# Group means of a four-layer image kernel: from a matmul with a matrix of means to block turns and sums on VectorE

## The reference

```python
xg = x.reshape(B, H, W, GROUPS, C // GROUPS)
mean = jnp.mean(xg, axis=(1, 2, 4), keepdims=True)
var = jnp.var(xg, axis=(1, 2, 4), keepdims=True)
xg = (xg - mean) * jax.lax.rsqrt(var + EPS)
```

## Time and profile before

| | us |
|---|---|
| median of 3 runs | 160.66 |
| lowest and highest | 159.46, 163.44 |
| the profiled execution, its own time | 159.53 |
| its span in the trace | 157.7 |
| PE busy | 149.7 (95%) |
| DVE busy | 104.8 (66%) |
| ACT busy | 108.7 (69%) |
| POOL busy | 50.1 (32%) |

### The profile page before, as it was taken

One profiled execution on the slowest core, in us unless ns is written; L12 is line 12 of the kernel. 1 busy time (PEld: TensorE's weight loads), 2 busy tenths in 40 slices (PEclk: granted clock), 3 DMA queues, 4 the chain that ended last, 5 costly groups with the idle time before them and its releaser, 6 DMA issues.

```text
span 157.7 us, 3715 instructions
## 1 busy us (share of the span) xinstructions
PE 149.7 (95%) x1405; PEld 114.7 (73%) x1405; DVE 104.8 (66%) x265; ACT 108.7 (69%) x261; POOL 50.1 (32%) x115
## 2 busy tenths in 40 slices
PE   7989999999999999999989997999989999999992
PEld 4569889887777678766667765766677756799992
DVE  0577899999996898568956377639975611235543
ACT  3567979973688458983778942697358879567970
POOL 6467657534517442214020038010200050026100
PEclk9999999999999999999999999999999999999999
DMA  5960000000000000000000000000000020000003
GB/s 147 321 267 0 0 8 0 2 4 0 2 2 4 0 0 4 4 0 4 4 2 6 4 0 0 8 0 4 2 2 8 0 75 0 0 4 33 0 33 133
DMA packets 2800, 4.30 MB, mean 27 GB/s; under 512 B 352, under 2 KB 2272, under 8 KB 2784
## 3 DMA queue, kind: packets, MB, share of 16 engines
q1 hardware_dynamic: 2496, 3.87, 7.2%
q10 hardware_dynamic: 288, 0.21, 0.4%
HBM read 2.90 MB, written 1.05 MB: 25 GB/s over the span
## 4 chain that ended last, share of the span: by engine, by line
PE 71%; DVE 16%; ACT 5%; POOL 4%; issue 2%; DVEq 0%; ACTq 0%
PE psum L658 9%; PE psum L647 8%; PE psum L626 7%; DVE nmax L1148 6%; PE psum L573 4%; PE psum L553 3%; PE psum L685 3%; PE psum L699 3%; ACT pT L907 3%; PE psum L728 3%; PE psum L669 2%; PE psum L721 2%; PE psum L720 2%; PE psum L518 2%; PE psum L737 2%
## 5 line engine op out<-in xcount | busy, mean ns | idle before, releaser
L1148 DVE TENSOR_REDUCE nmax<-psum 128x4 f32<-128x1024 f32 x32 | 38.3, 1217 | 6.7 <-PE psum L626 6.7
L907 ACT ACTIVATE pT<-psum 128x1024 f32<-128x1024 f32 x32 | 31.6, 1027 | 4.7 <-PE psum L647 4.4
L626 PE MATMUL psum<-qk 16*128 16x256 f32 (+1 forms) x256 | 18.1, 397 | 0.0
L647 PE MATMUL psum<-qk 32*128 32x256 f32 (+1 forms) x256 | 18.0, 398 | 0.1
L332 POOL COPY zE<-zE 128x17 f32<-128x17 f32 x8 | 1.6, 198 | 46.1 <-ACT zE L924 46.1
L658 PE MATMUL psum<-pT,vaug_all 128*32 128x256 f32 x256 | 16.0, 383 | 0.0
L626 PEld LDWEIGHTS psum<-qk 16*128 16x128 f32 (+1 forms) x256 | 11.7, 184 | 4.4 <-DVE nmax L1148 1.5
L647 PEld LDWEIGHTS psum<-qk 32*128 32x128 f32 (+1 forms) x256 | 11.6, 184 | 3.9 <-issue 1.6
L326 POOL TENSOR_TENSOR rstd<-vare,half 128x1 f32<-128x1 f32 x16 | 9.5, 591 | 14.7 <-DVE vare L1101 14.7
L382 POOL TENSOR_SCALAR mv<-mv 128x1 f32<-128x1 f32 x16 | 6.0, 375 | 24.7 <-DVE mv L1088 24.6
L658 PEld LDWEIGHTS psum<-pT,vaug_all 128*32 128x32 f32 x256 | 7.3, 109 | 6.4 <-issue 2.2
(11 more groups left out here) (160 smaller groups left out, 352.5 us busy)
## 6 DMA issues: line engine op xcount, KB each, us to landing
out<-x SPq DMA_DIRECT2D x8, 128.0 KB, 1.9
tab<-in_weights SPq DMA_DIRECT2D x1, 708.0 KB, 7.8
tab<-in_weights SPq DMA_DIRECT2D x1, 576.0 KB, 5.4
x0T<-in_xT SPq DMA_DIRECT2D x4, 128.0 KB, 3.1
x0T<-in_xT_rest SPq DMA_DIRECT2D x1, 512.0 KB, 6.2
tab<-in_weights SPq DMA_DIRECT2D x1, 320.0 KB, 6.6
qk<-stage_all SPq DMA_DIRECT2D x16, 8.0 KB
tab<-in_weights ACTq DMA_DIRECT2D x1, 128.0 KB, 2.9
```

The source lines that it names most:

```text
L626: last = mm(bank[(b0, b1)[j // 2] + j % 2][:, u * TOK:(u + 1) * TOK], at[:, u, 0, :], at[:, :, 1, :], start=True, stop=True)
L647: last = mm(bank[(b0, b1)[j // 2] + j % 2][:, m * TOK:(m + 1) * TOK], at[:, m, 1, :], at[:, :, 0, :], start=True, stop=True)
L907: go(pT[g](i)[:, 2 * k:2 * k + 2].rearrange("p j m t -> p j (m t)"), pair(home["st", g, i][k]), ACT.Exp).then_inc(s["exp" + "EO"[g]], 1)
L1148: v.tensor_reduce(nmax2(i)[:, g, 2 * k:2 * k + 2, :], pair(home["sm", g, i][k]).rearrange("p j (u m) -> p j u m", u=TILES), AX.X, ALU.max, ...
```

## The change

The matrices `mean1` and `mean2` leave the table (128 columns each of the third and fourth load), and with them `gm1` and `gm2` leave PE. In their place DVE gets four calls per norm. `turned` transposes the 32 x 32 blocks of a 128 x 32 tile, of which only the two columns of mean and mean of squares hold data: each block of 32 channels comes to lie along the free dimension. `group_sum` adds over groups of 4 or 8 channels there, `group_scaled` divides by the size of the group, and `turned_back` reads each result 4 or 8 times over and transposes the blocks back, so that every channel has its group's values in SBUF tile `gm`. `variance` and `normalised` read that tile and no PSUM. The tile `mv` becomes 32 columns wide and is filled with zeros once. The bias of L2 is added as a sum of two tiles, the second a column read 256 times over. All five sequences and the choice of banks are written anew.

```diff
-        mv = [ring(f"mv{k}", [P, 2]) for k in (1, 2)]
+        mv_all = [sb(f"mv{k}", [P, SLOTS, 32]) for k in (1, 2)]
+        mv = [lambda i, k=k: mv_all[k][:, i % SLOTS] for k in range(2)]
+        mvT, gm = ([ring(f"{n}{k}", [P, 32]) for k in (1, 2)] for n in ("mvT", "gm"))
+        sumT, gT = ([ring(f"{m}{k + 1}", [P, 32 // n]) for k, n in enumerate((GROUP1, GROUP2))] for m in ("sumT", "gT"))
...
+                for k in range(2):
+                    gp.memset(mv_all[k][:, :, :], 0.0)
...
-                gp.tensor_scalar(x2b(i), x0T(i), b_out2[:, :], None, ALU.add).then_inc(s["x2b"], 1)
+                gp.tensor_tensor(x2b(i), x0T(i), b_out2[:, :].to_broadcast((P, TOK)), ALU.add).then_inc(s["x2b"], 1)
...
-            def gm1(i, *marks):
-                freed(*marks)
-                pe.wait_ge(s["ms1"], i + 1)
-                mm(bank[home["o0", i]][:, TOK:TOK + 2], w("mean1"), mv[0](i), start=True, stop=True).then_inc(s["gm1"], 1)
...
-            def gm2(i, *marks):
...
-                mm(bank[home["o1", i]][:, TOK:TOK + 2], w("mean2"), mv[1](i), start=True, stop=True).then_inc(s["gm2"], 1)
...
-                v.bn_aggr(mv[layer - 1](i), bn[layer - 1](i)).then_inc(s[f"mv{layer}"], 1)
+                v.bn_aggr(mv[layer - 1](i)[:, 0:2], bn[layer - 1](i)).then_inc(s[f"mv{layer}"], 1)
+
+            def turned(i, layer, *marks):
+                after(marks)
+                dve.wait_ge(s[f"ms{layer}"], i + 1)
+                v.transpose(mvT[layer - 1](i), mv[layer - 1](i)).then_inc(s[f"mvT{layer}"], 1)
+
+            def group_sum(i, layer, *marks):
+                after(marks)
+                dve.wait_ge(s[f"mvT{layer}"], i + 1)
+                n = (GROUP1, GROUP2)[layer - 1]
+                v.tensor_reduce(sumT[layer - 1](i), mvT[layer - 1](i).rearrange("p (k n) -> p k n", n=n), AX.X, ALU.add).then_inc(s[f"sumT{layer}"], 1)
+
+            def group_scaled(i, layer, *marks):
+                after(marks)
+                dve.wait_ge(s[f"sumT{layer}"], i + 1)
+                n = (GROUP1, GROUP2)[layer - 1]
+                v.tensor_scalar(gT[layer - 1](i), sumT[layer - 1](i), 1.0 / n, None, ALU.mult).then_inc(s[f"gT{layer}"], 1)
+
+            def turned_back(i, layer, *marks):
+                after(marks)
+                dve.wait_ge(s[f"gT{layer}"], i + 1)
+                n = (GROUP1, GROUP2)[layer - 1]
+                v.transpose(gm[layer - 1](i), gT[layer - 1](i).unsqueeze(2).to_broadcast((P, 32 // n, n))).then_inc(s[f"gm{layer}"], 1)
...
-                g = bank[home[f"o{layer - 1}", i]][:, TOK:TOK + 2]
+                g = gm[layer - 1](i)
...
-                mean_of_group = bank[home[f"o{k}", i]][:, TOK:TOK + 1]
-                v.tensor_scalar(xn[k](i), x0T(i), mean_of_group, rstd[k](i), ALU.subtract, ALU.mult
+                v.tensor_scalar(xn[k](i), x0T(i), gm[k](i)[:, 0:1], rstd[k](i), ALU.subtract, ALU.mult
```

More of the change, by code:

```diff
@@ L412, in _ @@
+            z_difference(7, ("a", 6)); z_sum(7)
         @block.tensor
@@ L792, in _ @@
+            om(4, 4, ("xout", 4)); om(5, 1, ("s3", 7)); om(6, 0); om(7, 4, ("xout", 5))
         @block.scalar
@@ L980, in _ @@
+            s3_out(4); s3_out(5); s3_out(6); s3_out(7, ("out_ps", 5))
         @block.vector
@@ new lines, in _ @@
+            group_scaled(0, 1); turned_back(0, 1); variance(0, 1); variance_eps(0, 1); turned(1, 1); nmax0_out(4)
+            sum0_out(3); values_folded(); normalised(0, 1); group_sum(1, 1); group_scaled(1, 1); x1_out(2)
+            turned_back(1, 1); variance(1, 1); variance_eps(1, 1); moments(2, 1); inv0_out(3); mean(2, 1); sum0_out(4)
+            normalised(1, 1); p0_scaled(3); inv0_out(4); turned(2, 1); p0_scaled(4); nmax1_out(0); mlp_folded()
+            nmax1_out(1); inv1_out(0); group_sum(2, 1); p1_scaled(0); x1_out(3); group_scaled(2, 1); moments(3, 1)
@@ new lines, in _ @@
+            turned_back(2, 1); variance(2, 1); variance_eps(2, 1); nmax0_out(5); pool0(7); inv1_out(1); mean(3, 1)
+            normalised(2, 1); p1_scaled(1); x2_out(0); moments(0, 2); mean(0, 2); sum0_out(5); turned(3, 1)
+            group_sum(3, 1); inv0_out(5); group_scaled(3, 1); turned(0, 2); turned_back(3, 1); group_sum(0, 2)
+            group_scaled(0, 2); turned_back(0, 2); variance(0, 2); variance_eps(0, 2); nmax1_out(2); variance(3, 1)
+            normalised(0, 2); x2_out(1); x1_out(4); variance_eps(3, 1); moments(1, 2); moments(4, 1); mean(1, 2)
@@ new lines, in _ @@
+            nmax0_out(6); inv1_out(2); normalised(3, 1); turned(1, 2); p1_scaled(2); group_sum(1, 2); out2_folded()
+            group_scaled(1, 2); turned_back(1, 2); mean(4, 1); p0_scaled(5); nmax2_out(0, 0, 0); variance(1, 2)
+            nmax2_out(0, 0, 1); variance_eps(1, 2); nmax1_out(3); turned(4, 1); normalised(1, 2); nmax2_out(0, 1, 0)
+            group_sum(4, 1); group_scaled(4, 1); nmax2_out(0, 1, 1); turned_back(4, 1); inv1_out(3); variance(4, 1)
+            variance_eps(4, 1); x2_out(2); p1_scaled(3); normalised(4, 1); nmax2_out(1, 1, 0); x1_out(5); sum0_out(6)
@@ new lines, in _ @@
+            moments(2, 2); inv0_out(6); p0_scaled(6); nmax2_out(1, 1, 1); moments(5, 1); mean(5, 1); mean(2, 2)
+            nmax1_out(4); turned(5, 1); group_sum(5, 1); turned(2, 2); group_scaled(5, 1); group_sum(2, 2)
+            group_scaled(2, 2); turned_back(2, 2); variance(2, 2); variance_eps(2, 2); x1_out(6); moments(6, 1)
+            normalised(2, 2); turned_back(5, 1); variance(5, 1); x2_out(3); inv1_out(4); variance_eps(5, 1)
+            moments(3, 2); p1_scaled(4); normalised(5, 1); mean(3, 2); nmax2_out(1, 0, 0); nmax2_out(1, 0, 1)
@@ new lines, in _ @@
+            turned(3, 2); group_sum(3, 2); nmax1_out(5); nmax2_out(2, 1, 0); group_scaled(3, 2); turned_back(3, 2)
+            x2_out(4); nmax2_out(2, 1, 1); nmax0_out(7); mean(6, 1); variance(3, 2); moments(4, 2); variance_eps(3, 2)
+            sum0_out(7); turned(6, 1); group_sum(6, 1); group_scaled(6, 1); turned_back(6, 1); inv0_out(7)
+            normalised(3, 2); p0_scaled(7); mean(4, 2); nmax2_out(2, 0, 0); oinv_out(0); on_out(0); turned(4, 2)
+            inv1_out(5); variance(6, 1); variance_eps(6, 1); nmax2_out(2, 0, 1); normalised(6, 1); x1_out(7)
```

242 lines of the change are left out of this document (110 added, 132 removed).

## The result

| | before | changed |
|---|---|---|
| median us | 159.53 | 161.20 |
| lowest and highest | 159.16, 163.44 | 160.84, 163.80 |
| executions | 16 | 16 |
| profiled execution, its span | 159.53, 157.7 | 161.26, 159.4 |

The changed kernel takes 1.0097 times as long, 95% interval 1.0072 to 1.0121: slower by 1.0%. The forecast was 159.6, against the 160.66 shown, and a profiled execution 1.0 us quicker than before's; it became 1.7 us slower.

A forecast was written before the change was run, and what follows sets the result against it. PE, busy 95% of 157.7 us, was taken to set the length, with DVE also full from 20 to 46 us. Span 56.5 + 99.4 + 2.2 - 0.4 - 1.0 = 156.7 us, execution 158.5, predicted median 159.6, range 155.5 to 163.5.

The forecast's parts named there:

- the 4.5 us for the calls: DVE up to the maxima of image 1: nine norms at 0.5 us more each, 4.5 us more work.
- No wait for `z_sum(1)`, 1.0 us: POOL: `z_sum(1)` directly after the difference ends the wait of `am(1)`, 1.0 us gained.
- The last maxima of image 1: DVE ahead of `nt(1)`: 56.0 + 2.7 more work - 2.3 of waits gone, so done at 56.4 us.
- No wait of PE for a transfer behind `nt(1)`: Between `nt(1)` and `st(1, 1)`: about 2.5 us of PE work covers the transfer, priced at 0, up to 1.4 in the range.
- the credits ahead of `nt(1)`: DVE up to the maxima of image 1: 2.3 us of waits gone and 1.8 us less of other work.
- `nt(1)` right behind the maxima, 56.5: PE at image 1: `nt(1)` starts at 56.5 us instead of 58.3, directly after DVE's last maxima.
- The cover behind `nt(1)`: From `nt(1)` to the end: additional DVE work mostly covered, read from DVE busy 32.9 of 60 us between 80 and 140.
- PE's removed work behind `nt(1)` and the bank, put at 1.4 us: PE behind `nt(1)`: five group matmuls take 1.0 us away, a bank wait ahead of an `o1` 0.4.
- The price per norm: DVE: four calls of 0.69 us, less 0.08 overlap and 0.13 for `variance`, cost 0.5 us more; bounds 0.3 to 1.2.
- The banks' 3 us behind `nt(1)`: Rival, chance 0.37: banks freed earlier remove 3 us more of PE's waits behind `nt(1)`; median 156.6, 2.5% faster.
- DVE as the bound up to image 3: Rival, chance 0.15: norms cost DVE 1.0 us or more each, `nt(1)` starts at 61.0, median 164.1, 2.1% slower.
- 3.2 us of matmuls: PE: sixteen group matmul calls at 0.2 us each leave, 2.2 us ahead of `nt(1)` and 1.0 behind.

The follow-up runs named there:

- The kernel without calls: Changed kernel without the four DVE calls of each norm, group means left out, against the changed kernel: 156.80 us, 0.9809 of before, span 155.0.
- the kernel with all norms by turns and freed banks: Kernel before, old order: group matmuls replaced by the four DVE calls, six PE bank waits on x1 or x2: 165.84 us, 1.038 of before, span 164.0.
- the one without calls, to which 1.0 is added: Kernel before, old order, without group matmuls or DVE calls, banks freed, `z_sum(1)` earlier: 157.77 us, 0.9888 of before, span 155.4.
- The calls on spare tiles: Kernel before, group matmuls kept, plus four dependent DVE calls on unread tiles behind each `normalised`: 167.34 us, 1.0501 of before, span 165.5.
- the kernel with four late norms by turns: Kernel before with earlier `z_sum(1)`, second norms of images 4 to 7 by the four DVE calls, their banks freed: 159.16 us, 0.9974 of before.
- The kernel with the projections moved: Changed kernel with L0 projections of images 4 and 5 moved behind `p0t(0)` and `fold_biases2` on PE: 163.91 us, 1.0205 of before.

## Why the prediction was wrong

**Where the sum went wrong.** The span was forecast at 156.7 us and is 159.4. Of these 2.7 us 0.9 stand at `nt(1)`, which I put right behind the maxima, and 1.8 behind it, where I took DVE's additional work as covered. The kernel without calls shows a third error that the sum hides: without the 4.5 us for the calls the sum gives 152.2, and that kernel ends at 155.0. The 4.5 us, priced for nine norms, are by luck what all sixteen cost, 4.4. What was too large is the gain from everything else, by 2.8 us.

**The balance, in spans.** Removing the sixteen matmuls gives about 0.5 us, freed banks and `z_sum(1)` 1.8 more (157.7 to 155.4), the new order 0.4 (155.0), the four calls take 4.4 (159.4). In the old order they take 164.0 - (155.4 + 1.0) = 7.6: the kernel with all norms by turns and freed banks, against the one without calls, to which 1.0 is added because only it has the earlier `z_sum(1)`; that this move is worth 1.0 there too is an estimate from the run that has it alone. The calls on spare tiles took 7.8. So the new order hides about 3.2 us of the calls' cost, and that is not enough to make them pay.

**Right.** PE and DVE both full from 20 to 46 us in the kernel before. DVE's busy time and the number of instructions. No wait for `z_sum(1)`, 1.0 us. The last maxima of image 1, at 56.48 us against 56.4, were right by luck, as follows. The bias sum worth nothing. No wait of PE for a transfer behind `nt(1)`.

**The step that failed first: the credits ahead of `nt(1)`.** "Its waits between 46 and 56 us, 2.3 us, I take as gone", and 1.8 us of DVE work moved behind. The reason that I gave, waits for a PE that was ahead in its own work, fits only half of them. What DVE waited for in the kernel before (in us, times, longest; up to 58 us, of which between 46 and 56 lie all of the first and third line and the 0.8 of the second):

```profile
DVE xn L1110 <- POOL rstd L326: 1.1, 2, 0.7
DVE x0T L1076 <- PE psum L518: 1.1, 3, 0.8
DVE nmax L1148 <- PE psum L626: 0.3, 1, 0.3
```

Of the 2.2 us in this stretch half is for POOL's share of the norm. Without the price of the calls the two credits put the last maxima at 56.4 - 4.5 = 51.9 us; the kernel without calls has them at 53.7, and its DVE is still idle for 1.5 us from 46 to 56:

```profile
46.00:56.00 10.00, 10.00 (x98) 7.25 (x97) 8.47 (x20) 7.62 (x18) 3.50 (x9) 1.00 0.01 2
```

PE is busy for all of this stretch. At the last maxima of image 1 DVE waits for PE's scores, 0.89 us against 0.26 in the earlier trace rows:

```profile
51.33 2.35 DVE L1163 TENSOR_REDUCE nmax<-psum 128x4 f32<-128x1024 f32 x2 [0.89 <-PE psum L616]
```

With DVE's work lighter PE comes to the fore, and DVE waits for it. I had counted as a gain what exists only as long as the other engine is not reached. The calls fill part of it: with them 0.6 us of idle time are left, and the maxima come 2.8 us later for nine norms, not 4.5. The credits were 1.8 us too large and the calls 1.7 us too dear at that point, and the two cancel in the 56.4.

**`nt(1)` right behind the maxima, 56.5.** It came at 57.44. Before, an `sm` and an `o1` lay between the maxima and `nt(1)`, which started 2.3 us behind them; the new order takes the `o1` away, and I took the place as empty. The `sm` that PE starts at 56.36 was still there. In the kernel without calls the distance is the same 0.96 us. In all three kernels `nt(1)` comes when PE's own order reaches it. The point at which I joined the two engines was not one where they meet: they met at the normalised images and at x1, where PE waited. This step is 0.9 us of the sum.

**The cover behind `nt(1)`.** "Additional DVE work is mostly covered" was read from the stretch from 80 to 140 us and applied from 57 on. Seven norms stand there; those up to `nt(4)` cost 1.5 us, and all of them 1.6: from `nt(1)` to the end the changed kernel takes 102.0 us and the one without calls 100.4. The forecast had 100.2. So this is nearly all of the other 1.8 us. PE's removed work behind `nt(1)` and the bank, put at 1.4 us, gave 0.8 in the old order (97.6 us from `nt(1)` to the end instead of 99.4, less 1.0 for `z_sum(1)`); that the new order makes up for the rest is not shown.

**The price per norm.** 0.5 us was too low: four calls of 0.78, `variance` no shorter. With my 0.08 of overlap that is 0.69; DVE's busy time, which leaves the gaps out, rose by 9.7 us or 0.61 a norm. How such calls overlap shows in the timeline of the changed kernel:

```profile
48.74 0.20 DVE L1085 STREAM_TRANSPOSE mvT<-mv 128x32 f32<-128x32 f32 x1
48.98 0.18 DVE L1091 TENSOR_REDUCE sumT<-mvT 128x8 f32<-128x32 f32 x1
49.08 0.20 DVE L1085 STREAM_TRANSPOSE mvT<-mv 128x32 f32<-128x32 f32 x1
49.20 0.16 DVE L1097 TENSOR_SCALAR gT<-sumT 128x8 f32<-128x8 f32 x1
```

The sum needs the transposition ahead of it and starts 0.24 us after it; the next transposition belongs to another norm and starts 0.10 us after the sum, which lasts 0.18. The Trainium skill ("VectorE: DVE Perf Modes", section "The DRAIN you can't avoid") says that the next instruction does not start until the pipe is empty, and that one which is not held starts earlier. Here the dependent ones start after the end of the one ahead and the other one before it, as in the earlier trace rows.

**The rivals.** The banks' 3 us behind `nt(1)` did not come: with the norms on time they gave about 0.8 us (2.3 us of span for matmuls, banks and `z_sum(1)` together, less 0.5 and 1.0, if the three add up). Where the norms are late, in the old order with all calls, they gave 2.6 to 3.2. DVE as the bound up to image 3 was nearer the truth than I gave it credit for: in the kernel before it is as full there as PE, and the bound as soon as PE has less to do, as the 0.5 us for the removed matmuls shows; only the price stayed under 1.0 us.

Open: how much of the calls' cost in the new order is occupation of DVE and how much the longer way to the normalised image; why moving the scaling to POOL gave 0.7 us and not more is told by the 1.6 us of new waits only in part, and the loss of 0.8 us between `nt(4)` and `nt(7)` in the kernel with four late norms by turns was not followed further. Group matmuls inside the new order weren't tried; its banks are written again too early for them.

## What to carry to other kernels

Before pricing what leaves an engine, take it out and put nothing in its place: 3.2 us of matmuls on an engine 95% busy were worth 0.5. Eleven of the sixteen calls stood ahead of 58 us, six of them between 20 and 46 us, where the other engine was full too. A wait of engine A for engine B is no gain to be booked if B keeps its pace, and what A waits for has to be looked up: half of it was for a third engine. And look for the small thing in a large change: one moved call of POOL, worth 1.0 us by itself, beat the change as a whole.

## What the runs showed of the hardware

Small calls of DVE lasted about 0.2 us whatever they did: 0.20 us for a 128 x 32 transposition of blocks, 0.18 for a sum of it, 0.16 and 0.23 for a scaling of 4 and of 8 columns. The one-column `variance`, with two columns as operands, took 0.27 us from SBUF and 0.28 from PSUM.

The granted clock of TensorE fell to half, the 1.2 GHz level, for some 3 to 7 us in the profiles of six runs, each time soon after PE had waited in pieces of 0.5 to 1.2 us. The changed kernel waited 1.17 and 0.74 us at 32 to 34 us and kept 1.00 in its profile, so such waits do not always bring it about. The kernel with the projections moved, by stretches of 2 us:

```profile
8.00:10.00 2.00, 1.12 (x10) 0.95 (x10) 1.16 (x5) 1.85 (x7) 0.62 (x2) 1.00 0.97 379
10.00:12.00 2.00, 1.31 (x7) 0.99 (x7) 1.12 (x5) 1.05 (x4) 1.26 (x4) 0.71 0.23 92
12.00:14.00 2.00, 2.00 (x6) 1.73 (x7) 0.42 (x1) 0.07 (x1) 0.02 (x1) 0.50 0.02 8
14.00:16.00 2.00, 2.00 (x9) 1.83 (x8) 1.64 (x8) 0.93 (x3) 1.15 (x3) 0.50 0.00 0
```

PE had idle time in the two stretches from 8 to 12 us; in the second the clock falls, and from 12 us on it is 0.50. It fell a second time at 38 us. That execution took 167.9 us, the one at full clock 162.2, so that up to 5.7 us go with the clock. That the waits are what lowers it is suggested by the order of events in six profiles, not tested by a run.
